# Four PSUM banks in place of two for twelve maxima pieces, and a head mask made earlier, in a decoder block on one core

## The chip, the cores and the metric

One Trainium2 chip, of which the kernel uses one core. The metric is the device time of one execution in microseconds (us). A core has TensorE (PE, matmuls; PEld is its weight load), VectorE (DVE), ScalarE (ACT), GpSimd (POOL) and SyncE (SP, which here only issues DMAs). They run side by side, each through its own list of instructions in order, and meet at semaphores. Matmuls write to PSUM, which has eight banks of 128 x 512 f32.

## The reference

The reference is a decoder block over x (1 x 2048 x 256) with a context of 1601 rows, in f32:

```
h = x @ W_in.T + b_in                      # then a scan over the 2048 positions:
s = s * decay + B_p * h_t ; y_t = C_p * s  # per column, decay = exp(-softplus(log_A))
x = layernorm(x + gamma * norm(y @ W_out.T + b_out) + beta)
q, k, v = x @ Wq, ctx @ Wk, ctx @ Wv       # 8 heads of 64
x = layernorm(x + softmax(q k^T / 8) v @ Wo + bo)
x = layernorm(x + shared_mlp(x) + routed_experts(x))   # 16 experts, top 1
```

## The kernel before

The program has three stages: `before_attention`, `attention`, and the experts with the shared layer. Only the first is touched; it takes about the first 103 us. The attention works on 16 steps (4 chunks of 512 queries by 4 pairs of heads) and subtracts from each score row its maximum. The maxima of a step are found a step ahead, so the maxima for step 0 are made in the first stage, in 32 *pieces*.

In `before_attention` TensorE makes the input projection (L392, 8 groups) while ACT adds the bias (L245) and DVE runs the scan (L320). After that all engines walk through the same list of slots, the function `slots`: 33 slots t = 0, 1, 2, ..., and in each slot each engine does its own part of the named jobs, in a fixed order:

- `out` (t = 0 to 15): the output projection of tile t on TensorE (L403) in banks 2 and 3 by turns; DVE adds the bias (L336, which frees the bank, semaphore `v_z`) and makes the statistics (L338, L339): `norm_a`.
- `norm_b` of tile t - 5 on DVE (L346 to L351), `shifts` (L356), `norm_c` on ACT (L278), `tr`: the transpose of tile t - 12 on TensorE (L439).
- `key` or `val`, one unit per slot for t = 0 to 28, in the order of the list `kv`: slots 0 to 3 keys 0 to 3, slots 4 to 11 values 0 to 7, slots 12 to 15 keys 4 to 7, then keys and values by turns, and keys 13, 14, 15 in slots 26 to 28. Keys go through banks 4 and 5 (L415), ACT rounds them to `K_hi` (L252), DVE subtracts to `K_lo` (L328, `low`), and key n waits for `K_lo` of n - 2 (`v_klo`). Values go through banks 6 and 7 (L426) and ACT copies them out (L257, semaphore `a_v`). The last value is unit 12, in slot 25.
- `query` in slot 16: the query projection of step 0 (L445), `Q_hi` and `Q_alone` on ACT, `Q_lo` on DVE (L363). Before `Q_lo`, DVE makes `mask` (L361): it waits for 32 on `d_ident`, the semaphore of two loads, `ident` (L160) and `wq` (L161), and adds two 128 x 4 strips of `ident`. The mask is first read in the attention stage (L663).
- `piece`: one matmul of 128 x 400 (or 402) on TensorE (L459), and one maximum over it on DVE (L368, `piece_maximum`). From slot 17 on there is a piece ahead of the key or value and one behind it, from slot 24 on (`THREE_FROM`) a third at the slot's end. So slot 26 holds pieces 20, 21, 22, slot 27 pieces 23, 24, 25, slot 28 pieces 26, 27, 28, slot 29 pieces 29, 30, 31.

Pieces alternate between banks 3 (even) and 2 (odd), and piece n waits for the maximum of piece n - 2:

```
if n >= 2:
    pe.wait_ge(v_mx0, n - 1)
pe.matmul(banks[2 + (n + 1) % 2][:, 0:kn], Q_alone[:, h, i * P:(i + 1) * P], ...
```

When all 32 maxima are made, DVE reduces them to `nm` (L374). TensorE goes over to the attention's list: the query projection of step 1 (L773, which waits for `K_lo` of key 15), then the transpose of `nm` (L760, which waits for L374). `M` on DVE (L663) and the first scores (L806) come from it.

The SP queue issues the loads of this stage in this order: `w_in`, `xT`, `w_out`, the four rows, `wk`, `ctxT`, `xring`, `wv`, `xring`, `ident`, `wq`.

Of the kernel before, what the change touches and what calls it, by code (L numbers as in the profile page):

```python
# [9 lines left out]
ALU = mybir.AluOpType  # L10
ACT = mybir.ActivationFunctionType
AX = mybir.AxisListType

P = 128
# [5 lines left out]
KT = (KEYS + P - 1) // P  # L20
LAST = KEYS - (KT - 1) * P
HEADS, DH = 8, 64
# [4 lines left out]
QT = QC // P  # L27
# [5 lines left out]
KC = [(0, 402), (402, 400), (802, 400), (1202, 400)]  # L33


def by_head(nm, par):
    return nm[:, par].rearrange("p (h x) -> p h x", h=2)[:, :, 0:QT]


def before_attention(nc, io, mem):  # L40
# [4 lines left out]
    K_hi, K_lo, V, ident = mem["K_hi"], mem["K_lo"], mem["V"], mem["ident"]  # L45
    with ExitStack() as ctx:
        def sb(name, shape, dt=F32):
            return ctx.enter_context(nc.sbuf_tensor(name, shape, dt))

        def sem(name):  # L50
            return ctx.enter_context(nc.semaphore(name))
# [21 lines left out]
        x1T, mxp, nm, wq, mask = mem["x1T"], mem["mxp"], mem["nm"], mem["wq"], mem["mask"]  # L73
        Q_hi, Q_lo = mem["Q_hi"][0], mem["Q_lo"][0]
        Q_alone = sb("Q_alone", [P, 2, QC], F32R)
        banks = [ctx.enter_context(nc.psum_tensor(f"bank_a{i}", [P, 512], F32)) for i in range(8)]
# [4 lines left out]
        d_ident = sem("d_ident")  # L81
# [13 lines left out]
        p_v, a_v = sem("p_v"), sem("a_v")  # L95
# [4 lines left out]
        p_mx0, v_mx0, v_nm0 = sem("p_mx0"), sem("v_mx0"), sem("v_nm0")  # L100
# [6 lines left out]
              + [u for n in range(8, KT) for u in (("k", n), ("v", n))] + [("k", n) for n in range(KT, 16)])  # L107
        PIECES = TILE_U * len(KC)
        THREE_FROM = 24

        def slots(out=None, key=None, val=None, norm_b=None, shifts=None, norm_c=None, tr=None, query=None, piece=None,
                  low=None):


            def do(f, n, end):
                if f and 0 <= n < end:
                    f(n)

            pieces = iter(range(PIECES))
            for t in range(len(kv) + 4):  # L120
                do(out, t, TILES)
                if t == 16:
                    do(query, 0, 1)
                do(norm_b, t - 5, TILES)
                if t % 4 == 1:
                    do(shifts, (t - 9) // 4, G)
                do(norm_c, t - 10, TILES)
                do(tr, t - 12, TILES)
                if t > 16:
                    do(piece, next(pieces, -1), PIECES)  # L130
                if t < len(kv):
                    kind, u = kv[t]
                    do(key if kind == "k" else val, u, 16)
                if t > 16:
                    do(piece, next(pieces, -1), PIECES)
                if t < len(kv) and kv[t][0] == "k":
                    do(low, kv[t][1], 16)
                if t >= THREE_FROM:
                    do(piece, next(pieces, -1), PIECES)
# [153 lines left out]
        def vector_part(dve):  # L293
            links = [0]

            def link(ins):
                links[0] += 1
                ins.then_inc(v_link, 1)
                dve.wait_ge(v_link, links[0])

            dve.wait_ge(d_cols, 16)
            dve.wait_ge(a_exp, 1)
            dve.tensor_tensor(bB[:], cols[:, 0], cols[:, 2], ALU.mult).then_inc(prep, 1)

            dve.tensor_scalar(decay[:, 1], decay[:, 0], 1.0, None, ALU.add).then_inc(prep, 1)
            dve.wait_ge(prep, 2)
            dve.reciprocal(decay[:, 2], decay[:, 1]).then_inc(prep, 1)

            dve.wait_ge(prep, 3)
            for n in range(8):  # L310
                c, e = n // 2, n % 2
                if n == SCALE_AT:
                    dve.wait_ge(d_rows, 80)
                    for k in range(DK):
                        dve.tensor_scalar(w_out[:, k], w_out[:, k], cols[:, 3, k:k + 1], None, ALU.mult).then_inc(prep, 1)
                dve.wait_ge(a_u, n + 1)
                if c:
                    dve.wait_ge(v_scan, n - 1)
                u = state[:, e, c * 512:(c + 1) * 512]
                dve.tensor_tensor_scan(u, decay[:, 2, e:e + 1].to_broadcast([P, 512]), u,  # L320
                                       state[:, e, c * 512 - 1:c * 512] if c else 0.0,
                                       ALU.mult, ALU.add).then_inc(v_scan, 1)

            def key_low(n):
                p, j = kunits[n]
                k0, kn = KC[j]
                dve.wait_ge(a_khi, n + 1)
                dve.tensor_tensor(K_lo[:, p, k0:k0 + kn], banks[4 + n % 2][:, 0:kn], K_hi[:, p, k0:k0 + kn].bitcast(F32),  # L328
                                  ALU.subtract).then_inc(v_klo, 1)

            def norm_a(t):

                if t == 0:
                    dve.wait_ge(d_rows, 80)
                dve.wait_ge(p_out, t + 1)
                dve.tensor_tensor(z[:, t], banks[2 + t % 2][:, 0:D], rows[:, 0, :], ALU.add).then_inc(v_z, 1)  # L336
                dve.wait_ge(v_z, t + 1)
                link(dve.bn_stats(stats[:, t % 4, 0, :], z[:, t]))  # L338
                dve.bn_aggr(mv[:, 0, t], stats[:, t % 4, 0, :]).then_inc(v_mv1, 1)  # L339

            def norm_b(t):

                if t % 4 == 0:
                    dve.wait_ge(g_rstd1, t // 4 + 1)
                dve.wait_ge(g_xb, t + 1)
                link(dve.scalar_tensor_tensor(z[:, t], z[:, t], mv[:, 0, t, 0:1], rows[:, 1, :], ALU.subtract, ALU.mult))  # L346
                dve.scalar_tensor_tensor(z[:, t], z[:, t], rstd[:, 0, t:t + 1], xring[:, (t // 4) % 2, t % 4],
                                         ALU.mult, ALU.add).then_inc(v_b, 1)
                dve.wait_ge(v_b, t + 1)
                link(dve.bn_stats(stats[:, t % 4, 1, :], z[:, t]))  # L350
                dve.bn_aggr(mv[:, 1, t], stats[:, t % 4, 1, :]).then_inc(v_mv2, 1)  # L351

            def shifts(g):
                dve.wait_ge(g_rstd2, g + 1)
                tiles = slice(4 * g, 4 * g + 4)
                dve.scalar_tensor_tensor(shift[:, tiles], mv[:, 1, tiles, 0], -1.0, rstd[:, 1, tiles], ALU.mult, ALU.mult  # L356
                                         ).then_inc(v_shift2, 1)

            def query_low(_):
                dve.wait_ge(d_ident, 32)  # L360
                dve.tensor_tensor(mask[:], ident[:, 0:QT], ident[:, DH:DH + QT], ALU.add).then_inc(mem["v_mask"], 1)  # L361
                dve.wait_ge(a_q0, 3)
                dve.tensor_tensor(Q_lo[:], banks[1][:], Q_hi[:].bitcast(F32), ALU.subtract).then_inc(v_q0, 1)  # L363

            def piece_maximum(n):
                dve.wait_ge(p_mx0, n + 1)
                u, j = n // len(KC), n % len(KC)
                dve.tensor_reduce(mxp[:, 0, u, j:j + 1], banks[2 + (n + 1) % 2][:, 0:KC[j][1]], AX.X, ALU.max  # L368
                                  ).then_inc(v_mx0, 1)

            slots(out=norm_a, low=key_low, norm_b=norm_b, shifts=shifts, query=query_low, piece=piece_maximum)
            dve.wait_ge(v_mx0, PIECES)
            dve.wait_ge(g_const, 2)
            dve.tensor_reduce(by_head(nm, 0), mxp[:, 0].rearrange("p (h i) j -> p h i j", h=2), AX.X, ALU.max, negate=True  # L374
                              ).then_inc(v_nm0, 1)
            dve.wait_ge(v_nm0, 1)

        def tensor_part(pe):
# [69 lines left out]
            def piece(n):  # L448

                u, j = n // len(KC), n % len(KC)  # L450
                h, i = u // QT, u % QT
                k0, kn = KC[j]
                if n == 0:
                    pe.wait_ge(v_z, TILES)
                    pe.wait_ge(a_q0, 3)
                    pe.wait_ge(a_khi, len(KC))
                if n >= 2:
                    pe.wait_ge(v_mx0, n - 1)
                pe.matmul(banks[2 + (n + 1) % 2][:, 0:kn], Q_alone[:, h, i * P:(i + 1) * P], K_hi[:, 0, k0:k0 + kn],  # L459
                          start=True, stop=True).then_inc(p_mx0, 1)  # L460

            slots(out=out_proj, key=key, val=val, tr=transpose, query=query, piece=piece)

        return sync_part, gpsimd_part, scalar_part, vector_part, tensor_part


# [1470 lines left out]
```

## Time and profile before

| what | value |
|---|---|
| median of 3 runs | 881.26 us (881.13 to 881.49) |
| the profiled execution: its own time | 881.37 us |
| its span in the trace | 879.6 us |
| granted TensorE clock over the span | 0.995 |
| PE busy | 855.2 us (97%) |
| DVE busy | 568.5 us (65%) |
| ACT busy | 363.2 us (41%) |
| POOL busy | 562.8 us (64%) |

All times below count from the start of the span. A row of the timeline gives the start, the length, the engine, the line, the output and the input; "x4" says that four instructions are merged in it, and the bracket at its end gives the idle time of the engine just before and what ended it. A PE row's length includes a pipeline's end that overlaps with the next matmul. Rows of windows give, for each engine, its busy time and its number of instructions in the stretch.

### The profile page before, as it was taken

What the parts mean: (1) busy time and instruction counts of PE and PEld (TensorE: products, weight loads), DVE (VectorE), ACT (ScalarE), POOL (GpSimd) and SP (SyncE); (2) the same over time, 40 slices, a digit from 0 to 9 for tenths busy, and PEclk for the clock granted to TensorE, in tenths of its full rate; (3) what the DMA queues carried; (4) which work ended last, traced back from release to release, by engine and by line L of the source; (5) the groups of instructions that cost most, each with busy time, mean ns of one, the idle gap of its engine ahead of it and who ended that gap; (6) DMA issues with size and microseconds to landing.
All of it is one profiled execution on the core that took longest, in us unless ns stands there. A gap on an engine that the chain in (4) does not pass through costs nothing.

```text
span 879.6 us, 12720 instructions
## 1 busy us (share of the span) xinstructions
PE 855.2 (97%) x4798; PEld 505.5 (57%) x4798; DVE 568.5 (65%) x1149; ACT 363.2 (41%) x510; POOL 562.8 (64%) x366
## 2 busy tenths in 40 slices
PE   9998899999999999999999999999999999999994
PEld 4654555555555455555455556554478898885441
DVE  4798757667666677676677675774677746335553
ACT  3254344434435445443445443544446224323332
POOL 0354298898896898896988986989400153333444
PEclk9999999999999999999999999999999999999998
DMA  9213300000001100000100000104079211484420
GB/s 266 76 48 99 118 1 1 25 1 1 1 1 36 37 1 1 1 1 3 45 25 1 1 1 1 48 1 168 7 178 354 92 49 49 144 282 121 130 71 23
DMA packets 44140, 55.12 MB, mean 63 GB/s; under 512 B 3624, under 2 KB 35120, under 8 KB 44080
## 3 DMA queue, kind: packets, MB, share of 16 engines
q1 hardware_dynamic: 37840, 46.16, 16.7%
q0 software_dynamic: 2688, 6.31, 2.0%
q10 hardware_dynamic: 3552, 1.84, 0.7%
q8 instruction: 39, 0.64, 0.3%
q14 instruction: 21, 0.17, 0.1%
HBM read 36.44 MB, written 18.89 MB: 63 GB/s over the span
## 4 chain that ended last, share of the span: by engine, by line
PE 90%; DVE 7%; issue 1%; POOL 1%; ACT 1%; POOLq 0%; DVEq 0%
PE st L806 24%; PE av L828 21%; PE mx L792 8%; PE bg L1442 4%; PE bu L1442 4%; PE bt L1451 4%; PE bgu L1731 3%; PE misc L773 3%; PE misc L845 2%; PE bank_a L392 2%; PE bank_a L415 1%; PE bgu L1728 1%; PE br L1451 1%; PE mx L859 1%; PE misc L859 1%; PE by L1731 1%
## 5 line engine op out<-in xcount | busy, mean ns | idle before, releaser
L611 POOL TENSOR_TENSOR accG<-accG,probs 128x1024 f32<-128x1024 f32 (+1 forms) x170 | 405.0, 2383 | 38.8 <-ACT probs L633 23.8
L633 ACT ACTIVATE probs<-st 128x1024 f32<-128x1024 f32 (+1 forms) x208 | 212.6, 1025 | 203.2 <-PE st L806 197.5
L678 DVE TENSOR_REDUCE mxp<-mx 128x1 f32<-128x512 f32 x360 | 232.0, 686 | 60.1 <-PE mx L792 54.5
L828 PE MATMUL av<-probs,V 128*64 128x512 f32 (+1 forms) x832 | 191.7, 598 | 0.0
L792 PE MATMUL mx<-K_hi,Q_hi 64*128 64x512 f32 (+1 forms) x480 | 137.9, 380 | 0.0
L828 PEld LDWEIGHTS av<-probs,V 128*64 128x64 f32 (+1 forms) x832 | 55.5, 136 | 105.7 <-issue 83.9
L806 PE MATMUL st<-Q_hi,K_hi 64*128 64x512 f32 (+1 forms) x416 | 112.9, 444 | 0.9 <-ACT probs L633 0.9
L792 PEld LDWEIGHTS mx<-K_hi,Q_hi 64*128 64x128 f32 x480 | 73.8, 184 | 51.8 <-issue 26.8
L806 PE MATMUL st<-M,ones_r 64*128 64x512 f32 (+1 forms) x416 | 101.2, 393 | 0.0
L806 PE MATMUL st<-Q_hi,K_lo 64*128 64x512 f32 (+1 forms) x416 | 96.6, 393 | 0.0
L806 PE MATMUL st<-Q_lo,K_hi 64*128 64x512 f32 (+1 forms) x416 | 94.5, 394 | 0.0
L806 PEld LDWEIGHTS st<-Q_hi,K_hi 64*128 64x128 f32 (+1 forms) x416 | 48.2, 179 | 46.3 <-ACT probs L633 31.3
L693 DVE RECIPROCAL misc<-misc 128x128 f32<-128x128 f32 x64 | 61.4, 960 | 6.3 <-PE misc L845 6.3
L611 POOL TENSOR_TENSOR accG<-probs 128x1024 f32<-128x1024 f32 x16 | 38.4, 2397 | 27.5 <-ACT probs L633 27.5
L806 PEld LDWEIGHTS st<-M,ones_r 64*128 64x128 f32 (+1 forms) x416 | 50.8, 180 | 7.5 <-DVE M L663 0.7
L806 PEld LDWEIGHTS st<-Q_lo,K_hi 64*128 64x128 f32 (+1 forms) x416 | 49.5, 181 | 3.8
L806 PEld LDWEIGHTS st<-Q_hi,K_lo 64*128 64x128 f32 (+1 forms) x416 | 47.5, 180 | 6.2
L1129 POOL DMA_INDIRECT scratch_sorted_x<-x2s,pos x16 | 17.0, 1060 | 37.6 <-DVE pos L1286 23.7
L1442 PE MATMUL bg<-x2T_high,wgate_cut 128*128 128x512 f32 x128 | 40.2, 395 | 0.3 <-DVE h_raw L1312 0.3
L1442 PE MATMUL bu<-x2T_high,wup_cut 128*128 128x512 f32 x128 | 40.0, 394 | 0.0
L675 DVE TENSOR_REDUCE mxp<-mx 128x4 f32<-128x264 f32 x30 | 11.7, 431 | 39.0 <-PE mx L792 39.0
L638 ACT ACTIVATE o_raw<-av 128x512 f32<-128x512 f32 x16 | 9.6, 597 | 60.8 <-PE av L828 60.8
(259 smaller groups left out, 1305.7 us busy)
## 6 DMA issues: line engine op xcount, KB each, us to landing
w_gate_up<-in_gate_up SPq DMA_DIRECT2D x4, 2048.0 KB
w_down<-in_down SPq DMA_DIRECT2D x2, 2048.0 KB, 9.6
scratch_sorted_x<-zero SPq DMA_DIRECT2D x6, 514.0 KB, 8.2
xs<-scratch_sorted_x SPq DMA_DIRECT2D x24, 128.5 KB, 2.3
scratch_base<-zero SPq DMA_DIRECT2D x6, 512.0 KB, 9.4
base<-scratch_base SPq DMA_DIRECT2D x24, 128.0 KB, 2.1
xring<-in_x SPq DMA_DIRECT2D x4, 512.0 KB, 8.9
scratch_x1b<-xT SPq DMA_DIRECT2D x4, 512.0 KB, 2.9
```

The source lines that it names most:

```text
L392: mm = pe.matmul(banks[n % 2][:], w_in[:, k, e * P:(e + 1) * P], xT[:, k, c * 512:(c + 1) * 512], start=(k == 0), stop=(k == DK - 1))
L611: pool.tensor_tensor(total[0:r], so_far[0:r], probs[0:r, place(S, t)], ALU.add).then_inc(g_add, 1)
L633: act.activation(probs[0:r, place(S, t)], st[g % 2][0:r, :], ACT.Exp, scale=DH ** -0.5).then_inc(a_probs, 1)
L678: dve.tensor_reduce(mxp[:, F % 2, h * QT + i, j:j + 1], mx[h][:, 0:kn], AX.X, ALU.max).then_inc(v_mx, 1)
L693: dve.reciprocal(misc[:, cols], misc[:, cols]).then_inc(v_rsum, 1)
L773: mm = pe.matmul(misc[:], wq[:, k, pair * P:(pair + 1) * P], x1T[:, k, :], start=(k == 0), stop=(k == DK - 1))
L792: mm = pe.matmul(mx[h][:, a * kn:(a + 1) * kn], Q_hi[F % 2][rows, q * P:(q + 1) * P], K_hi[rows, F % PAIRS, k0:k0 + kn], start=True, stop= ...
L806: mm = pe.matmul(st[g % 2][0:r, h * QC:(h + 1) * QC], w, q, start=(part == 0), stop=(part == MAXIMA))
L828: mm = pe.matmul(av[h * DH:(h + 1) * DH, :], V[0:r, t, (2 * p + h) * DH:(2 * p + h + 1) * DH], probs[0:r, place(S, t), h * QC:(h + 1) * QC ...
L1442: mm = pe.matmul(bank[f % 2][:], wp[:, k, f * P:(f + 1) * P], xp[:, k, cols], start=(k == n == 0), stop=(k == DK - 1 and n == len(products ...
L1451: return pe.matmul(sum_bank(c * QT + i)[:, 0:D], h, (wd_high, wd_low, wd_high)[n][:, f, :], start=(f == n == 0), stop=(f == FK - 1 and n = ...
L1731: pe.matmul(out[0:HALF, 0:cols], rows_T[:, k * P:k * P + HALF], chosen_rows, start=(k == 0), stop=(k == DK - 1))
```

## The change

Two edits in `before_attention`.

1. Pieces 20 to 31 go round the banks 6, 7, 3, 2 in place of 3 and 2. Piece 20 waits until all 13 values are copied out of banks 6 and 7 (`a_v`); pieces 22 to 31 wait for the maximum of piece n - 4 in place of n - 2. Pieces 0 to 19 are as before.
2. The mask, with its wait for `d_ident`, is made by DVE ahead of the slots, so right behind the scan and ahead of `norm_a` of tile 0, in place of in slot 16.

```diff
         THREE_FROM = 24
+        FOUR_FROM = 20
+
+        def piece_bank(n):
+            return banks[2 + (n + 1) % 2] if n < FOUR_FROM else banks[(6, 7, 3, 2)[n % 4]]
...
             def query_low(_):
-                dve.wait_ge(d_ident, 32)
-                dve.tensor_tensor(mask[:], ident[:, 0:QT], ident[:, DH:DH + QT], ALU.add).then_inc(mem["v_mask"], 1)
                 dve.wait_ge(a_q0, 3)
...
-                dve.tensor_reduce(mxp[:, 0, u, j:j + 1], banks[2 + (n + 1) % 2][:, 0:KC[j][1]], AX.X, ALU.max
+                dve.tensor_reduce(mxp[:, 0, u, j:j + 1], piece_bank(n)[:, 0:KC[j][1]], AX.X, ALU.max
                                   ).then_inc(v_mx0, 1)
 
+            dve.wait_ge(d_ident, 32)
+            dve.tensor_tensor(mask[:], ident[:, 0:QT], ident[:, DH:DH + QT], ALU.add).then_inc(mem["v_mask"], 1)
             slots(out=norm_a, low=key_low, norm_b=norm_b, shifts=shifts, query=query_low, piece=piece_maximum)
...
-                if n >= 2:
+                if n == FOUR_FROM:
+                    pe.wait_ge(a_v, KT)
+                if n >= FOUR_FROM + 2:
+                    pe.wait_ge(v_mx0, n - 3)
+                elif 2 <= n < FOUR_FROM:
                     pe.wait_ge(v_mx0, n - 1)
-                pe.matmul(banks[2 + (n + 1) % 2][:, 0:kn], Q_alone[:, h, i * P:(i + 1) * P], K_hi[:, 0, k0:k0 + kn],
+                pe.matmul(piece_bank(n)[:, 0:kn], Q_alone[:, h, i * P:(i + 1) * P], K_hi[:, 0, k0:k0 + kn],
                           start=True, stop=True).then_inc(p_mx0, 1)
```

## Rows read from the trace of the kernel before

**Rows 1.** The page: the chain that ended last, shares of the span.

```profile
PE 90%; DVE 7%; issue 1%; POOL 1%; ACT 1%; POOLq 0%; DVEq 0%
```

**Rows 2.** DVE's timeline, from the scan's end to the first norm_b.

```profile
22.47 0.42 DVE L336 TENSOR_TENSOR xT<-bank_a,x 128x256 f32<-128x256 f32 x1
...
24.29 0.58 DVE L328 TENSOR_TENSOR K_lo<-bank_a,K_hi 128x402 fp32r<-128x402 f32 x1 [0.71 <-ACT K_hi L252]
...
33.81 0.42 DVE L336 TENSOR_TENSOR xT<-bank_a,x 128x256 f32<-128x256 f32 x1 [1.32 <-PE bank_a L403]
...
34.83 0.48 DVE L346 SCALAR_TENSOR_TENSOR xT<-xT,mv,x 128x256 f32<-128x256 f32 x1
```

**Rows 3.** TensorE's timeline, key 1, output projection 2 and key 2.

```profile
24.41 1.51 PE L415 MATMUL bank_a<-ctxT,wk 128*128 128x400 f32 x4
25.75 1.02 PE L403 MATMUL bank_a<-w_out,state 128*128 128x256 f32 x4
26.62 1.51 PE L415 MATMUL bank_a<-ctxT,wk 128*128 128x400 f32 x4
```

**Rows 4.** The DMA queue's timeline, and issues with KB and us to landing.

```profile
19.27 0.44 SPq L161 DMA_DIRECT2D wq<-in_wq x1
```

```profile
wq<-in_wq SPq DMA_DIRECT2D x1, 512.0 KB, 8.5
ident<-in_ident SPq DMA_DIRECT2D x1, 64.0 KB, 12.8
```

**Rows 5.** DVE's and POOL's timelines: a small DVE operation alone, and the mask.

```profile
6.68 0.16 DVE L303 TENSOR_TENSOR bB<-cols 128x2 f32<-128x2 f32 x1 [6.68 <-ACT decay L240]
...
23.57 5.59 POOL L207 TENSOR_TENSOR xring<-xring,x 128x256 f32<-128x256 f32 x8 [20.59 <-DMA xring<-in_x]
...
65.13 0.56 DVE L361 TENSOR_TENSOR mask<-ident 128x4 f32<-128x4 f32 x1
65.61 0.68 DVE L363 TENSOR_TENSOR Q_lo<-bank_a,Q_hi 128x512 fp32r<-128x512 f32 x1
```

**Rows 6.** TensorE's timelines, matmuls and weight loads: slot 16 and the pieces' end.

```profile
66.44 0.41 PE L439 MATMUL bank_a<-ident,xT 128*128 128x128 f32 x2 [2.46 <-DVE Q_lo L363]
...
91.65 0.19 PEld L459 LDWEIGHTS bank_a<-K_hi,Q_alone 128*128 128x128 f32 x1 [0.50 <-DVE mxp L368]
91.95 1.50 PE L415 MATMUL bank_a<-ctxT,wk 128*128 128x400 f32 x4
92.98 0.84 PE L459 MATMUL bank_a<-K_hi,Q_alone 128*128 128x400 f32 x2
...
94.30 0.45 PE L459 MATMUL bank_a<-K_hi,Q_alone 128*128 128x400 f32 x1 [0.26 <-DVE mxp L368]
...
101.32 1.88 PE L773 MATMUL misc<-x1T,wq 128*128 128x512 f32 x4
103.03 0.27 PE L760 MATMUL mx<-ident,nm 128*128 128x128 f32 x1
```

**Rows 7.** ACT's and DVE's timelines, slots 25 to 29.

```profile
90.84 0.59 ACT L257 ACTIVATE V<-bank_a 65x512 f32<-65x512 f32 x1 [1.75 <-PE bank_a L426]
...
93.67 0.57 DVE L368 TENSOR_REDUCE mxp<-bank_a 128x1 f32<-128x400 f32 x1 [0.95 <-PE bank_a L459]
94.16 0.56 DVE L328 TENSOR_TENSOR K_lo<-bank_a,K_hi 128x400 fp32r<-128x400 f32 x1
...
102.13 0.19 DVE L374 TENSOR_REDUCE nm<-mxp 128x8 f32<-128x32 f32 x1
```

**Rows 8.** Windows of 1 us: length, PE, PEld, DVE, ACT, POOL busy, PEclk, DMA share, GB/s.

```profile
65.00:66.00 1.00, 0.00 (x0) 0.00 (x0) 1.00 (x3) 0.53 (x2) 1.00 (x2) 1.00 0.00 0
867.00:868.00 1.00, 0.87 (x8) 0.30 (x4) 0.70 (x3) 0.00 (x0) 0.70 (x2) 1.00 0.11 38
870.00:871.00 1.00, 0.00 (x0) 0.00 (x0) 0.16 (x1) 0.04 (x1) 0.72 (x1) 0.90 0.18 66
```

**Rows 9.** TensorE's timeline: the first matmuls of the run.

```profile
1.24 4.64 PE L381 MATMUL bank_a<-nm 128*128 128x256 f32 x10 [1.24 <-POOL nm L183]
```

## The prediction

> **What bounds the kernel now.** I read the chain that ended last first. It lies 90% on TensorE and 7% on DVE [rows 1]. The attention and the experts are TensorE's, and the change does not touch them; they follow the first stage at a fixed distance, since their first scores hang on the transpose of `nm`, which starts at 103.03 us [rows 6]. So the question is only by how much that transpose moves.
>
> Then I read the engines' timelines of the first 103 us, and found three stretches with different limits.
>
> From 21 to 34 us TensorE sets the pace. It goes without a pause through output projections and keys, 2.21 us from key 1 to key 2 [rows 3], and DVE waits in each slot: 0.71 us before K_lo of key 0, 1.32 us before norm_a of tile 5 [rows 2].
>
> From 33.81 us, when norm_a of tile 5 starts, to about 80 us DVE runs without any idle time (its rows carry no bracket there), and TensorE is held by DVE, by 2.46 us before the transpose in slot 16 [rows 6]. What delays norm_a of tile 5 delays all of this, and what DVE saves in it comes back.
>
> From about 86 us both engines wait for each other in turn: TensorE for a maximum ahead of the first piece of a slot (0.50 us of idle weight load at 91.65), DVE for the piece behind the key (0.95 us at 93.67) [rows 6, 7]. That is the latency of a loop over two banks, not work.
>
> **The mask's wait, step by step.** Today DVE goes from the last scan straight into norm_a of tile 0, at 22.47 [rows 2]. The change puts a wait for both loads of `d_ident` there. The later is `wq`: issued at 19.27, landed 8.5 us on, so at 27.77; `ident` takes 12.8 us in a queue that moves it no sooner than 26.4 [rows 4]. Today the same wait stands in slot 16 and costs nothing. So DVE will stand still from 22.47 to about 27.85 (0.06 to 0.08 for the semaphore). Queued behind it are norm_a of tile 0 and K_lo of key 0, and TensorE waits for both: output projection 2 needs the bank that norm_a of tile 0 frees, key 2 the one that K_lo of key 0 frees. TensorE still has output projection 1 and key 1 to do, which end at 24.41 + 1.51 = 25.92 [rows 3]. That much of the stall is covered, the rest is not.
>
> The mask itself: bounds are 0.16 us, the length of a small operation with nothing beside it, and 0.48, from 65.13 to the next operation in slot 16, where POOL's adds ran beside it [rows 5]. At 27.8 POOL is adding too (23.57 to 29.16) [rows 5], so I take 0.48. norm_a of tile 0 starts its first operation at 27.85 + 0.48 = 28.33, and that ends 0.42 later, at 28.75. TensorE starts output projection 2 at 28.81 (0.06 for the semaphore) in place of 25.75, so 3.06 us late. DVE then needs 1.02 us for norm_a (33.81 to 34.83) and 0.58 for K_lo of key 0 [rows 2]: 28.33 + 1.02 + 0.58 = 29.93, and key 2 starts at 29.99 in place of 26.62, 3.37 us late. From there TensorE is the slower one again: output projection 3, 1.34 later at 31.33, finds its bank free since 30.25, and key 3, due at 32.20, finds K_lo of key 1 done at 31.43. So the delay stays 3.37, and norm_a of tile 5 starts at 37.18 in place of 33.81. The 1.32 us that DVE idles before it can't take it up, because that wait is for TensorE, which is late by the same amount; from there on DVE has no idle time to give back. **Term 1: +3.37 us** (3.05 with the small mask).
>
> POOL's first inverse square root needs norm_a of tile 3, done at about 33.9, and is through well before 38.2, when norm_b of tile 0 wants it. The second pair of `xring` loads waits for norm_b and shifts with it; SP has nothing else that waits for DVE.
>
> **The mask taken out of slot 16.** 65.13 to 65.61 is 0.48 us of DVE's unbroken stretch, right ahead of `Q_lo`, for which TensorE waits [rows 5, 6]. **Term 2: -0.48 us**; bounds 0 and 0.48.
>
> **Four banks for pieces 20 to 31.** Times here are those of the kernel before, without the shift. Piece 20, at 91.65 now, will wait for the last value's copy, 90.84 + 0.59 = 91.43 [rows 6, 7], and start at 91.49. Its key follows 0.30 later, piece 21 another 1.03 later [rows 6], at 92.82. A slot now takes 2.65 us (91.65 to 94.30), with the 0.50 of idle weight load in it [rows 6]; each piece now asks for a maximum two further back, so that wait falls away, and the slot takes 2.14. DVE needs 0.49 for a maximum and about as much for a K_lo (93.67 to 94.16) [rows 7], so 1.96 a slot. The two are nearly equal, and the end is DVE's. The maximum of piece 21 comes 0.69 behind it as now (92.98 to 93.67), at 93.51. Piece 24 starts at 94.96, its maximum at 95.65; piece 27, a slot later that has no transpose and so takes about 2.0, at 96.97, its maximum at 97.66. Behind that DVE has no wait left: K_lo of key 15 and maxima 28 to 31. Maximum 31 starts at 97.66 + 5 x 0.49 = 100.11 and ends 0.57 later at 100.68; `nm` runs from 100.71 for 0.19 us [rows 7] to 100.90, and the transpose starts at 100.96. TensorE's query projection needs K_lo of key 15 (98.7) and then 1.71 us (101.32 to 103.03) [rows 6], so it is through before. 103.03 - 100.96 gives **Term 3: -2.07 us**. Bounds: if DVE never waited after 93.51, 13 x 0.49 would bring maximum 31 to 99.88, so 2.3; if half of what TensorE gains comes back as waits for DVE, 1.0.
>
> The stores of `x1b` that the first exponent waits for hang on the last transposes, which move as little as piece 20 does; SP has seen them landed by 99.8 already now, so they are covered, by some 3 us.
>
> **Sum.** 3.37 - 0.48 - 2.07 = +0.82 us. The profiled execution took 881.37 (span 879.6 and 1.8 around it), so it would take 882.19; it lies 0.11 above the median, so the median would be 882.1.
>
> **The clock in the gap.** Between key 1 and output projection 2 TensorE will stand idle from 25.92 to 28.81, 2.89 us. The longest such gap now is 2.46 us before 66.44, and the granted clock reads 1.00 in it, the 2.4 GHz level [rows 6, 8]. After the last matmul, which ended at 867.87, it fell to the 1.2 GHz level within the window 870 to 871, whose mean is 0.90, so at about 870.8, after 2.9 us [rows 8]. The Trainium skill (TensorE: Matmul & The Clock Gate, "Part 1: The HAM clock gate") says that half rate is the default state and that activity lifts it, so that an idle array falls back. By it the stall could cost more than its length; by the row of 66.44 it costs only that.
>
> **Rivals.**
>
> *The clock falls in the gap* (18%). For: 2.9 us at the end of the span was enough. Against: 2.46 us was not, and this gap is only as long as the one that just sufficed. Price: TensorE sets the pace right behind it. At the start of the run ten matmuls took 4.64 us, 0.46 each, where four of the same shape later take 1.02, 0.26 each [rows 9, 3]; so the low level lasted at least those 4.6 us, and half of them, 2.3 us, is what such a spell costs; one of half that length costs 1.2. That adds up to 883.3 to 884.4. It decides from 0.9 us of loss on: then the kernel is slower by over 0.2%.
>
> *The stall counts whole* (7%): nothing covers it, 28.33 - 22.47 = 5.86 in place of 3.37, so 884.6. For: DVE is late by that. Against: TensorE has work until 25.92, and DVE waits for it in every slot [rows 2, 3].
>
> *The four banks bring little* (10%): DVE becomes the bound at once, or banks 6 and 7 are free later; term 3 is -1.0, and the time 883.1. Against: DVE's 0.95 us of idle at 93.67 [rows 7].
>
> *The stall is short* (7%): the load of `wq` lands when the scan ends, or soon after. Then only the gain is left, 881.26 - 2.1 = 879.2; with half of the stall, 880.7. Against: 27.77 in this trace [rows 4].
>
> **How the numbers follow.** The forecast holds 58%. 0.2% is 1.76 us, about what a measurement of this kernel can tell from no change. Its own range: landing half a microsecond either way, mask 0.16 to 0.48, term 3 from -2.3 to -1.5, so 881.0 to 883.2. The range of 8 in 10 takes in the clock's case, so 880.7 to 884.5. Slower than 883.0: the clock 18, the whole stall 7, half of the little banks, a tip of the forecast, so 31%. Faster than 879.5: 5%. The rest, 64%, is within.
>
> **What would show it.** In the changed trace: the mask at about 27.8 with an idle bracket of over 5 us before it, ended by the load of `wq`; output projection 2 near 28.8 and key 2 near 30.0; norm_a of tile 5 near 37.2; the transpose in slot 16 2.9 us later than now; the rows of the pieces in slots 27 to 29 with no bracket; DVE unbroken from the maximum of piece 27 to `nm`; the transpose of `nm` near 103.85. The lengths of the matmuls from 28.8 to 34 tell whether the clock fell, even if its column does not. The prediction is wrong if the wait ends elsewhere than 27 to 28.5, if norm_a of tile 5 is not 3.4 late, or if the stages behind the transpose change their distance.

## The result and the profile after

The changed kernel takes 884.59 us (median of 6 runs, 883.23 to 885.97), before 881.29 (881.13 to 881.61) on the same chip: a ratio of 1.0032, 95% interval 1.0022 to 1.0042. It is slower, by 3.3 us by the two medians and by 2.8 by the ratio. The forecast was 882.1, with "within 0.2%" (883.0 or less) as the likeliest; that likeliest outcome did not come. The time lies at the upper end of the range of 880.7 to 884.5 (the median is 0.1 above it, the ratio puts it at 884.1, inside), where the rival with the falling clock had its place. The profiled execution took 884.75, with a span of 882.9. Of all runs below one is in a slower state, 896.79 us at a mean clock of 0.942, and is left aside.

DVE's timeline of the kernel after, the stretch of [rows 2]:

```profile
28.22 0.70 DVE L374 TENSOR_TENSOR mask<-ident 128x4 f32<-128x4 f32 x1 [6.08 <-DMA wq<-in_wq]
28.84 0.41 DVE L340 TENSOR_TENSOR xT<-bank_a,x 128x256 f32<-128x256 f32 x1
...
29.85 0.54 DVE L332 TENSOR_TENSOR K_lo<-bank_a,K_hi 128x402 fp32r<-128x402 f32 x1
...
39.41 0.42 DVE L340 TENSOR_TENSOR xT<-bank_a,x 128x256 f32<-128x256 f32 x1 [1.32 <-PE bank_a L407]
```

The mask stands behind 6.08 us of waiting for `wq`. norm_a of tile 5 is at 39.41 in place of 33.81 [rows 2]: 5.60 us late, not 3.37. (In the eight profiled executions that have no stall this operation starts anywhere from 33.36 to 34.63, so a lateness against the one profile of before is good to about half a microsecond. Distances inside one trace, such as from the mask to norm_a of tile 5, don't carry this scatter.) TensorE's timeline of the same stretch, and windows of 1 us (columns as in [rows 8]):

```profile
24.77 1.51 PE L419 MATMUL bank_a<-ctxT,wk 128*128 128x400 f32 x4
29.40 1.10 PE L407 MATMUL bank_a<-w_out,state 128*128 128x256 f32 x4 [3.12 <-DVE xT L340]
30.45 3.04 PE L419 MATMUL bank_a<-ctxT,wk 128*128 128x400 f32 x4
33.28 1.31 PE L407 MATMUL bank_a<-w_out,state 128*128 128x256 f32 x4
34.42 1.51 PE L419 MATMUL bank_a<-ctxT,wk 128*128 128x400 f32 x4
```

```profile
29.00:30.00 1.00, 0.60 (x3) 0.58 (x4) 0.93 (x4) 0.00 (x0) 0.58 (x1) 1.00 0.00 0
30.00:31.00 1.00, 1.00 (x4) 0.60 (x3) 0.97 (x3) 0.00 (x0) 0.00 (x0) 0.71 0.00 0
31.00:32.00 1.00, 1.00 (x3) 0.39 (x2) 0.96 (x4) 0.00 (x0) 0.00 (x0) 0.50 0.00 0
32.00:33.00 1.00, 1.00 (x3) 0.62 (x2) 0.80 (x3) 0.00 (x0) 0.00 (x0) 0.50 0.00 0
33.00:34.00 1.00, 1.00 (x4) 0.60 (x3) 0.00 (x0) 0.48 (x1) 0.00 (x0) 0.58 0.00 0
```

TensorE was idle for 3.12 us. The gap is over at 29.40, and the granted clock still reads 1.00 there; it falls to the 1.2 GHz level at about 30.4 and returns at about 33.8. Key 2 lies in that spell and takes 3.04 us where key 3 takes 1.51.

The end of the pieces, TensorE's and DVE's timelines, where [rows 6, 7] stood before:

```profile
97.01 0.45 PE L467 MATMUL bank_a<-K_hi,Q_alone 128*128 128x402 f32 x1
97.30 1.51 PE L419 MATMUL bank_a<-ctxT,wk 128*128 128x400 f32 x4
98.34 0.84 PE L467 MATMUL bank_a<-K_hi,Q_alone 128*128 128x400 f32 x2
...
102.35 1.80 PE L467 MATMUL bank_a<-K_hi,Q_alone 128*128 128x400 f32 x5
104.27 1.96 PE L781 MATMUL misc<-x1T,wq 128*128 128x512 f32 x4
106.41 0.30 PE L768 MATMUL mx<-ident,nm 128*128 128x128 f32 x1 [0.19 <-DVE nm L378]
```

```profile
102.11 1.52 DVE L370 TENSOR_REDUCE mxp<-bank_a 128x1 f32<-128x400 f32 x3
103.56 0.56 DVE L332 TENSOR_TENSOR K_lo<-bank_a,K_hi 128x400 fp32r<-128x400 f32 x1
104.04 2.01 DVE L370 TENSOR_REDUCE mxp<-bank_a 128x1 f32<-128x402 f32 x4
106.08 0.19 DVE L378 TENSOR_REDUCE nm<-mxp 128x8 f32<-128x32 f32 x1
```

No piece waits any more, DVE runs through to `nm`, and the transpose of `nm` now waits for it (0.19 us). It starts at 106.41, 3.38 us later than the 103.03 of [rows 6], and the span is 3.3 us longer: nothing behind it changed its distance.

So the place of the time can be followed by four marks of the two traces: norm_a of tile 5 +5.60 (39.41 against 33.81), the transpose that waits for `Q_lo` +5.11 (71.55 against 66.44; it is the first work of slot 17, and what the prediction calls the transpose in slot 16), the last value +5.53 (94.45 against 88.92), the transpose of `nm` +3.38. I use the distance from the last value to that transpose for the banks (14.11 before, 11.96 after), and the one from norm_a of tile 5 to the last value for the stretch that DVE bounds (55.11 before, 55.04 after).

### The profile page after: what moved, and what is told of

Its sections match the earlier page's. It is cut to its first block, busy times and chain, and to the rows that moved or that the text cites. A ratio compares the mean times of both kernels' runs of the same rounds, so it can differ in the third digit from the quotient of the medians.

```text
span 882.9 us, 12720 instructions
## 1 busy us (share of the span) xinstructions
PE 856.7 (97%) x4798; PEld 506.0 (57%) x4798; DVE 568.2 (64%) x1149; ACT 363.4 (41%) x510; POOL 563.1 (64%) x366
## 4 chain that ended last, share of the span: by engine, by line
PE 86%; DVE 8%; SPq 2%; issue 1%; DMA 1%; ACT 1%; POOL 1%; POOLq 0%; DVEq 0%
PE st L814 24%; PE av L836 21%; PE mx L800 8%; PE bg L1450 4%; PE bu L1450 4%; PE bt L1459 4%; PE bgu L1739 3%; PE misc L781 3%; PE misc L853 2%; PE bgu L1736 1%; PE br L1459 1%; PE mx L867 1%; PE misc L867 1%; PE by L1739 1%; PE bank_a L419 1%
## 5 line engine op out<-in xcount | busy, mean ns | idle before, releaser
L800 PEld LDWEIGHTS mx<-K_hi,Q_hi 64*128 64x128 f32 x480 | 73.9, 184 | 51.9 <-issue 26.8
```

What stands on the lines that cost most here:

```text
L800: mm = pe.matmul(mx[h][:, a * kn:(a + 1) * kn], Q_hi[F % 2][rows, q * P:(q + 1) * P], K_hi[rows, F % PAIRS, k0:k0 + kn], start=True, stop= ...
```

## The experiments

Twelve kernels ran in three groups of four, each group on one chip beside the kernel before: its median was 881.80 us in the first group, 881.54 in the second, 881.62 in the third. "Fillers" are matmuls of L381's kind, on zeros and with results that nothing reads, put in where TensorE would stand idle (the trace shows each of these f32 matmuls as two, so six as x12):

```diff
+            def fill(times):
+                for _ in range(times):
+                    pe.matmul(banks[7][:, 0:D], nm[:, 0], nm[:, :, :].rearrange("p a n -> p (a n)"), start=True, stop=True)
```

### The two edits one at a time

**The four banks alone:**

```diff
             def query_low(_):
+                dve.wait_ge(d_ident, 32)
+                dve.tensor_tensor(mask[:], ident[:, 0:QT], ident[:, DH:DH + QT], ALU.add).then_inc(mem["v_mask"], 1)
                 dve.wait_ge(a_q0, 3)
...
-            dve.wait_ge(d_ident, 32)
-            dve.tensor_tensor(mask[:], ident[:, 0:QT], ident[:, DH:DH + QT], ALU.add).then_inc(mem["v_mask"], 1)
```

> The four banks alone, the mask left in slot 16. In the changed kernel the delay against before shrinks from 5.53 us at the last value to 3.38 us at the transpose of nm, so the banks give 2.15 us. Theory (the two edits add up): 881.3 - 2.15 = 879.1 us, transpose of nm near 100.9, granted clock full throughout. Rival (the banks only caught up time that the stall had lost, because DVE was bunched up): under 0.5 us gained, 880.8 or more.

Measured: 879.58 us (12 runs, 878.88 to 882.42), ratio 0.9974 (0.9964 to 0.9984), 2.2 us less than before. From the last value (89.36) to the transpose of `nm` (101.32) it is 11.96, as in the changed kernel. The banks' gain is their own. The clock fell once in this execution, behind a gap of 2.45 us in slot 17, and this time it cost nothing that the marks show (55.10 us from norm_a of tile 5 to the last value, 55.11 before):

```profile
66.88 0.41 PE L443 MATMUL bank_a<-ident,xT 128*128 128x128 f32 x2 [2.45 <-DVE Q_lo L367]
...
67.31 3.34 PE L430 MATMUL bank_a<-wv,ctxT 128*128 128x512 f32 x4
```

```profile
68.00:69.00 1.00, 1.00 (x3) 0.48 (x2) 0.94 (x3) 0.00 (x0) 0.81 (x2) 0.50 0.30 94
```

**The early mask alone,** pieces on two banks (the second edit applied to the kernel before):

> The early mask alone, pieces on two banks. Theory: the loss of norm_a of tile 5 (5.60 us in the changed kernel) less 0.49 for the freed slot 16, plus the 0.42 that DVE loses between slots 16 and 25: about +5.4, so 886.7 us, with a spread over the runs of 2 us or more as in the changed kernel, where before spreads 0.5. Rival (the loss is only the late load, without a clock effect): +3.4 to +3.9, so 885.0, spread 0.5.

Measured: 886.60 us (5 runs, 885.34 to 886.81), ratio 1.0047 (1.0034 to 1.0061), so +4.8 us in medians and +4.1 by the ratio, on five runs. The last value starts at 94.29, the distance to the transpose (108.40) is again 14.11, and its windows show the clock at 0.53, 0.50, 0.50, 0.77 from 30 to 34 us. +4.8 and -2.2 make +2.6; the changed kernel came to +2.8 (884.36 against 881.54) in the second group. The edits add up, within the half microsecond that these numbers allow. The spread, on which the expectation had leaned, is no sign of anything: that of the kernel before was 3.35 us on this chip.

### Is it the clock or the stall?

**The first gap filled:**

```diff
             def out_proj(t):
                 pe.wait_ge(v_scan, 2 * (t // 4 + 1))
+                if t == 2:
+                    for _ in range(6):
+                        pe.matmul(banks[7][:, 0:D], nm[:, 0], nm[:, :, :].rearrange("p a n -> p (a n)"), start=True, stop=True)
```

> The changed kernel with six more matmuls of the kind of L381 (128x256, on zeros, into bank 7, which is free then) between key 1 and output projection 2, to fill TensorE's gap; their results are not used. They take about 2.6 us of the gap of 3.1 us, so by themselves they cost nothing. Theory (the gap lets the granted clock fall, and slow matmuls cost 1.8 us behind it): clock 1.00 throughout, key 2 takes 1.51 us in place of 3.04, time 882.8 us with a spread of 0.6 or less. Rival (the stall's own length makes the whole loss): 884.6 us, no less, and the spread stays.

Measured: 883.38 us (12 runs, 882.28 to 884.82), ratio 1.0018 (1.0010 to 1.0027). The gap is filled, and TensorE's timeline has key 2 at its full speed:

```profile
25.52 2.75 PE L406 MATMUL bank_a<-nm 128*128 128x256 f32 x12
28.69 1.13 PE L410 MATMUL bank_a<-w_out,state 128*128 128x256 f32 x4 [0.41 <-DVE xT L340]
29.83 1.61 PE L422 MATMUL bank_a<-ctxT,wk 128*128 128x400 f32 x4
```

The median is 0.6 above the 882.8 of the theory, and the interval touches that of the changed kernel, so the trace carries this and not the time. The spread stayed, and in the profiled execution the clock fell later, from 75.0 to 78.4 us. That is behind a gap of 2.17 us before piece 2, which nobody had asked about.

**The changed kernel again,** for its spread and for the chip:

> The changed kernel unaltered, on the same chip as the next three. Theory (the clock falls in its first gap in most executions and in the gaps of slots 17 and 18 in some): 884.6 us, spread 2 us or more; it shows how the chip differs from the one of the first comparison.

Measured: 884.36 us (all twelve runs), ratio 1.0029 (1.0020 to 1.0037). Without 896.79 its eleven runs fall in two heaps, four from 882.56 to 883.21 and seven from 884.30 to 885.18. The profiled execution is one of the low heap. The program is that of the first profile, so only the execution and the chip differ. Its TensorE timeline:

```profile
28.43 1.10 PE L407 MATMUL bank_a<-w_out,state 128*128 128x256 f32 x4 [2.87 <-DVE xT L340]
29.48 1.61 PE L419 MATMUL bank_a<-ctxT,wk 128*128 128x400 f32 x4
30.93 1.03 PE L407 MATMUL bank_a<-w_out,state 128*128 128x256 f32 x4
```

The same gap, 0.25 us shorter at 2.87 us, and no fall behind it; key 2 takes 1.61. Its mask ran 0.99 us earlier (27.23 against 28.22, the landing of `wq`), norm_a of tile 5 came 2.63 earlier (36.78 against 39.41), so 1.64 is the clock. That this is what parts the two heaps is not shown: no high run of this series was profiled, and the mean clock over a run, which is on record for each, doesn't part them (0.991 to 0.994 in the low heap, 0.990 to 0.992 in the high one).

In slot 18 it is the other way round. A gap of 2.17 us stands before piece 2 in both executions. In the first the clock stayed at 1.00 behind it, and the key after it took 1.50; here it fell (0.50 from 75 to 78 us), and the key took 2.23. The first profile:

```profile
76.44 0.45 PE L467 MATMUL bank_a<-K_hi,Q_alone 128*128 128x400 f32 x1 [2.17 <-DVE mxp L370]
76.72 1.50 PE L419 MATMUL bank_a<-ctxT,wk 128*128 128x400 f32 x4
```

This one:

```profile
73.86 0.45 PE L467 MATMUL bank_a<-K_hi,Q_alone 128*128 128x400 f32 x1 [2.17 <-DVE mxp L370]
74.14 2.23 PE L419 MATMUL bank_a<-ctxT,wk 128*128 128x400 f32 x4
```

So the same gap in the same program keeps the clock in one execution and loses it in another. In the two profiles that kept it (this program's first and that of the early mask alone) the clock had already fallen once, at 30 us; whether that plays a part is not shown.

**All three gaps filled in the changed kernel:**

```diff
                 pe.wait_ge(v_scan, 2 * (t // 4 + 1))
+                if t == 2:
+                    fill(6)
...
                 if t == QT + 1:
+                    pe.wait_ge(a_v, 8)
+                    fill(5)
                     pe.wait_ge(v_q0, 1)
...
                     pe.wait_ge(a_khi, len(KC))
+                if n == 2:
+                    fill(3)
```

> The changed kernel with filling matmuls in all three gaps: six before output projection 2, five ahead of the transpose in slot 17, three ahead of piece 2; on zeros, into bank 7, results not used. Theory (with the clock held, what is left is the stall of 3.4 to 3.8, the banks' 2.15, and nothing from slot 16): the kernel before with held clock took 881.45, so 882.7 to 883.1, spread 1 us or less; the changed kernel without fillers 1.4 us more. Rival (the stall costs its full length whatever the clock does): 884.4 or more.

Measured: 883.17 us (11 runs, 882.30 to 884.18), ratio 1.0015 (1.0006 to 1.0024), with ten of the runs within 1.2 us. The changed kernel without fillers had 1.0029, so holding the clock gives back about 1.2 us in the median. The two intervals touch and the chips differ; the mean clock of the runs speaks for it too, 0.9915 over the eleven without fillers and 0.9946 over the eleven with them. norm_a of tile 5:

```profile
28.09 0.75 DVE L374 TENSOR_TENSOR mask<-ident 128x4 f32<-128x4 f32 x1 [5.95 <-DMA wq<-in_wq]
```

```profile
37.66 0.42 DVE L340 TENSOR_TENSOR xT<-bank_a,x 128x256 f32<-128x256 f32 x1 [1.32 <-PE bank_a L413]
```

37.66 with the mask at 28.09 is 3.85 us late against before. In the first profile the mask was 0.13 later and norm_a of tile 5 was 5.60 late, so the clock cost 1.62 there, the same as by the other pair.

**The kernel before with the fillers** of slots 17 and 18:

> The kernel before with filling matmuls in the two longest gaps of TensorE: five ahead of the transpose in slot 17 (gap 2.46 us) and three ahead of piece 2 (gap 1.74 us), on zeros, into bank 7, results not used. Theory (the scatter of 880.6 to 884.0 us of the kernel before on the last chip comes from executions in which the clock falls in these gaps, as it did at 67 us in the profile of the four banks alone): the high values of 882.4 and more go, the rest stays at 881.3 to 881.6. Rival (the scatter comes from the DMAs or elsewhere): the spread is as that of before.

Measured: 881.45 us (11 runs, 880.88 to 882.45), ratio 0.9997 (0.9988 to 1.0006). The fillers do what they are for: of the 31 runs of the kernel before beside it 16 have a mean clock of 0.992 or 0.993, with fillers none is below 0.994. But the median doesn't move, so in this kernel the falls cost nothing in most runs. Three of the 31 were at 883.64 to 883.79, and with fillers there is none above 882.45; three in 31 are too few for none in 11 to say anything.

### How long a stall costs what?

**The mask waits for `ident` alone:**

```diff
-            sp.dma_start(ident[:], io["ident"]).then_inc(d_ident, 16)
+            sp.dma_start(ident[:], io["ident"]).then_inc(d_id, 16)
...
-            dve.wait_ge(d_ident, 32)
+            dve.wait_ge(d_id, 16)
```

(with the fillers of slots 17 and 18, and the other waits split in the same way)

> The changed kernel where the mask, still ahead of tile 0, waits for the load of ident alone (a semaphore of its own), fillers in slots 17 and 18, none in the first gap. ident landed at 26.3 in the changed kernel's trace, wq at 28.2. Theory (the stall is set by the landing, and TensorE hides what lies before 25.9): the mask at 26.3, output projection 2 at about 27.4, 1.6 us late, key 2 1.9 late, gap of 1.5 us and no fall of the clock in it: 881.45 + 1.9 - 2.4 = 881.0, within 0.4. Rival (a wait of any length there costs a fall of the clock): 882.5 or more.

Measured: 881.84 us (11 runs, 880.99 to 884.30), ratio 1.0002 (0.9993 to 1.0011). `ident` landed at 26.8 in this execution, 0.5 later than I had put it:

```profile
26.85 0.62 DVE L374 TENSOR_TENSOR mask<-ident 128x4 f32<-128x4 f32 x1 [4.97 <-DMA ident<-in_ident]
```

```profile
27.95 1.10 PE L411 MATMUL bank_a<-w_out,state 128*128 128x256 f32 x4 [1.74 <-DVE xT L340]
29.00 1.61 PE L423 MATMUL bank_a<-ctxT,wk 128*128 128x400 f32 x4
```

A gap of 1.74 us, key 2 at full speed, norm_a of tile 5 at 36.30, 2.49 late: 881.45 + 2.49 - 2.15 = 881.8, which is the measured time, 0.4 above the range expected, and below the rival. Against the kernel with all gaps filled (mask at 28.09, norm_a of tile 5 3.85 late) a stall that ends 1.24 us earlier costs 1.36 less, and neither has a clock effect.

**The load of `ident` moved ahead of `w_out`,** with its own semaphore, no fillers:

```diff
+            sp.dma_start(ident[:], io["ident"]).then_inc(d_id, 16)
             sp.dma_start(w_out[:], io["w_outT"].rearrange("(k p) n -> p k n", p=P)).then_inc(d_rows, 16)
```

> The changed kernel with ident loaded right before w_out and with a semaphore of its own, so that the mask waits for ident alone and finds it there at 22.4. Theory (the whole loss hangs on the wait): the mask takes 0.2 to 0.6 us of DVE, which mostly disappears in the 0.71 us that DVE waits for K_hi of key 0; slot 16 gives 0.49, the banks 2.15; 881.3 - 2.6 + 0 to 0.4 = 878.7 to 879.1. Rival (putting the mask ahead of tile 0 costs its own time on the path from the scan): 879.3 or more. A second rival: the load moved forward delays w_out and the rows, and the scale of w_out and norm_a of tile 0 come later.

Measured: 879.92 us (12 runs, 879.11 to 883.41), ratio 0.9982 (0.9971 to 0.9993). The stall is gone, and the mask costs next to nothing:

```profile
21.62 0.14 DVE L374 TENSOR_TENSOR mask<-ident 128x4 f32<-128x4 f32 x1
21.69 0.43 DVE L340 TENSOR_TENSOR xT<-bank_a,x 128x256 f32<-128x256 f32 x1
```

0.07 us, where beside POOL's adds it took 0.62 (28.22 to 28.84). The median is 0.8 us above what I expected, and in the range of the rival; five of the twelve runs are at 880.67 or more. The profiled run is one of these. In it key 0 waited 1.33 us for `ctxT`, norm_a of tile 5 came at 34.63, and the clock fell behind a gap of 2.17 us (0.50 from 73 to 75 us; 55.59 us from norm_a of tile 5 to the last value). A kernel that leaves the loads as they were (the mask in slot 5 on two banks, below) had the same wait for `ctxT`, 1.20 us, so it can't be laid to the moved load; whether the moved load costs anything stays open.

**The mask in slot 5,** where DVE idles, with four banks:

```diff
                 if t == 0:
                     dve.wait_ge(d_rows, 80)
+                if t == 5:
+                    dve.wait_ge(d_ident, 32)
+                    dve.tensor_tensor(mask[:], ident[:, 0:QT], ident[:, DH:DH + QT], ALU.add).then_inc(mem["v_mask"], 1)
```

> Four banks, and the mask made in slot 5, ahead of norm_a of tile 5, where DVE idles 1.32 us and both loads landed 5 us before. Theory: no stall, no gap; the four banks give 2.15, slot 16 between 0 and 0.49 (with the mask gone from it, the next operation of DVE took 0.91 in place of 0.47 us in the changed kernel): 878.7 to 879.2 on a chip where before takes 881.3. Rival (the mask in slot 5 delays norm_a of tile 5, since DVE is full from there): 879.2 to 879.6.

Measured: 880.12 us (12 runs, 879.34 to 883.14), ratio 0.9986 (0.9977 to 0.9995). No stall; the mask takes 0.13 us in DVE's idle time. The chip's before is 881.54, so this is only 1.4 us less, and the four banks alone had given 2.2; both the theory and the rival had the time lower. In the profile (879.62 us) the clock falls at 72.0 and is back at 75.4, behind a gap that is longer than before:

```profile
66.02 0.41 PE L444 MATMUL bank_a<-ident,xT 128*128 128x128 f32 x2 [1.93 <-DVE Q_lo L368]
...
70.90 0.45 PE L468 MATMUL bank_a<-K_hi,Q_alone 128*128 128x400 f32 x1 [2.16 <-DVE mxp L373]
71.19 2.04 PE L420 MATMUL bank_a<-ctxT,wk 128*128 128x400 f32 x4
```

With the mask out of slot 16 the gap that ends with `Q_lo` shrinks from 2.46 [rows 6] to 1.93, and the one before piece 2 grows from 1.74 to 2.16.

**The same with fillers:**

> The version with the mask in slot 5 together with the same filling matmuls in slots 17 and 18. Theory: the low values of the version with the mask in slot 5, 878.7 to 879.2, without high ones; spread under 1 us. Rival: no difference from it, or slower by the fillers that run past the wait (up to 0.4 us).

Measured: 879.04 us (7 runs, 878.58 to 879.79), ratio 0.9971 (0.9960 to 0.9982), spread 1.2 us. This is the lowest ratio of all: 2.5 us less than before, 5.3 less than the changed kernel beside it. It is not told apart from the four banks alone without fillers (0.9974, 0.9964 to 0.9984): the second edit, put where it does no harm, gains nothing that these runs show.

### What slot 16 and the number of banks are worth

**The mask in slot 5 on two banks, with fillers:**

> The mask in slot 5 alone, on two banks, clock held: the worth of taking the mask out of slot 16 by itself, against 881.45 for the kernel before with held clock. Theory A (DVE's 0.48 us come back): 880.95. Theory B (POOL's adds beside slot 16 hold the next operation of DVE instead, 0.91 in place of 0.47 us, and nothing comes back): 881.4, and in the trace K_lo of the slot to the norm's statistics 2.41 us apart where it was 2.45.

Measured: 881.53 us (11 runs, 881.01 to 882.38), ratio 0.9998 (0.9989 to 1.0007), against 0.9997 with the mask in slot 16. DVE's timeline in slots 16 and 17, and POOL's beside it:

```profile
65.83 0.68 DVE L364 TENSOR_TENSOR Q_lo<-bank_a,Q_hi 128x512 fp32r<-128x512 f32 x1
66.42 0.92 DVE L349 SCALAR_TENSOR_TENSOR xT<-xT,mv,x 128x256 f32<-128x256 f32 x1
67.38 0.83 DVE L350 SCALAR_TENSOR_TENSOR xT<-xT,rstd,xring 128x256 f32<-128x256 f32 x1
68.24 0.43 DVE L353 BATCH_NORM_STATS2 stats<-xT 128x6 f32<-128x256 f32 x1
```

```profile
65.64 3.15 POOL L222 TENSOR_TENSOR xT<-xT,x 128x256 f32<-128x256 f32 x4
```

From `Q_lo` to the statistics it is 2.41 us; before, from the mask to the statistics, it was 2.45 (65.13 to 67.58). The first operation of norm_b takes 0.92 in place of 0.47. POOL's adds of 0.79 us each run beside both, and the time that the mask had taken longer, norm_b's first operation now takes longer. That is theory B, by the trace; the interval of the time would still hold theory A. That POOL's adds are what both wait for is read from their standing side by side: no run changed POOL.

**Three banks,** mask in slot 5, with fillers:

```diff
-            return banks[2 + (n + 1) % 2] if n < FOUR_FROM else banks[(6, 7, 3, 2)[n % 4]]
+            return banks[2 + (n + 1) % 2] if n < FOUR_FROM else banks[(3, 6, 7)[n % 3]]
...
-                if n >= FOUR_FROM + 2:
-                    pe.wait_ge(v_mx0, n - 3)
+                if n >= FOUR_FROM + 1:
+                    pe.wait_ge(v_mx0, n - 2)
```

> Mask in slot 5, clock held, and pieces 20 to 31 round three banks (3, 6, 7) in place of four: a piece waits for the maximum three back. Theory (the loss of the two banks was the latency of their loop, and one more bank covers it, as DVE is the bound from there on): 879.0 to 879.3, as with four (879.04). Rival (each bank gives its share): half of the 2.4 us, 880.2.

Measured: 879.74 us (11 runs, 879.25 to 882.63), ratio 0.9981 (0.9972 to 0.9990). From the last value (88.75) to the transpose (101.01) it is 12.26, with four banks 11.97 (88.52 to 100.49), with two 14.11. The third bank brings 1.85 of the 2.14, the fourth 0.29, because the last piece still waits with three:

```profile
99.01 0.45 PE L476 MATMUL bank_a<-K_hi,Q_alone 128*128 128x400 f32 x1 [0.52 <-DVE mxp L373]
```

The theory holds in its main part, though the time is 0.4 above its range; the times alone (0.9971 and 0.9981) would not tell three from four.

## Why the prediction came out as it did

The time came out at the upper end of the range, but by a case that I had given 18%: the forecast's own path gives 882.1, and its range ended at 883.2. By one of the prediction's own signs it was wrong, since norm_a of tile 5 was not 3.4 late; the other two (the wait's end, 28.2, and the stages behind the transpose) came as said. Point by point:

- **"The mask's wait, step by step", term 1, +3.37.** The mechanism was right: who waits, what TensorE covers, and that nothing is given back until DVE's stretch. It was 5.60. Of this 3.98 is the stall (3.85 with all gaps filled and the mask at 28.09, and 0.13 for the mask at 28.22): `wq` landed later (mask at 28.22, not 27.85, 0.37), the mask took 0.62 (not 0.48, 0.14), and TensorE started 0.15 behind norm_a's first operation (not 0.06); key 2 came at 30.45, not 29.99, and the rest is a tenth of a microsecond or two behind it. The other 1.62 is the clock. From the mask to norm_a of tile 5 it is 11.19 us in this profile and 11.03 in that of the early mask alone, where the clock fell, and 9.53, 9.55 and 9.57 in the three where it did not: 1.5 to 1.7 us, with nothing taken from the kernel before.
- **"The clock in the gap", by the row of 66.44 the stall "costs only that".** This is the step that failed. A gap of 2.46 us that had kept its clock in one profile was taken for a gap that always keeps it. The runs show that it is a matter of the execution: behind 2.45 us the four banks alone lost it (windows of 0.79 and three of 0.50 from 67 to 71 us), and behind 2.46 the kernel before kept it; behind 2.17 us in slot 18 the changed kernel lost it in one profile and kept it in another. In the first gap it was lost behind 3.12 and 3.08 us and kept behind 2.87; these three alone would also fit a limit on the length. Filled, key 2 ran at full speed in both profiles. The Trainium skill's rule (TensorE: Matmul & The Clock Gate, "Part 1: The HAM clock gate"), that activity lifts the clock and an idle array falls back, was right against my reading of the row: the trace agrees, with 0.50 from 31 to 33 us behind the gap. But the clock read 1.00 through the whole gap and fell a microsecond after work had begun again. The rival's price, 1.2 to 2.3 us, holds the measured 1.6: the spell lasted 3.4 us (30.4 to 33.8) at half the clock. The price had been taken from the lengths of the first matmuls of the run, where the clock's column reads 1.00 (from 1 to 6 us), so the column is no witness there. The chance was too low if anything, with a fall in two of the three profiles that have the long gap unfilled.
- **"The mask taken out of slot 16", term 2, -0.48.** Wrong: 0 to 0.1. The distance from norm_a of tile 5 to the last value is 55.04 after and 55.11 before. I had POOL's adds beside the mask in hand, and used them for the mask's price in its new place, but not for what is freed: where an operation is long only because of something that runs beside it, taking it out can free nothing, since the next one is long instead (0.92 in place of 0.47 us).
- **"Four banks for pieces 20 to 31", term 3, -2.07.** Right: 2.15, alone, with the early mask, and with the mask in slot 5. The details came as said: no brackets, DVE unbroken to `nm`, the transpose waiting for it.
- **The sum.** 3.98 + 1.62 - 0.07 - 2.15 = 3.38, the delay of the transpose; terms of 3.98 - 0.07 - 2.15 = +1.8 without the clock agree with 883.17, which is 1.6 above before. The forecast's sum of +0.82 missed the clock (1.62), 0.61 of stall and 0.41 of slot 16, and gained 0.08 by the banks: nearly all its errors lay on one side, and two thirds of the miss is the term that it put at nothing.
- **Behind the transpose** nothing moved: 776.57 us from it to the end of the span before, 776.49 after, 776.71 in the best version.

What stays open: the few runs 2 to 3 us above the rest, of the kernel before too. With fillers in slots 17 and 18 only two such runs are left in the 62 runs of the six series that have them (882.63 with three banks, 884.30 with the wait for `ident` alone). A single fall in the stretch that DVE bounds isn't enough for them. The distance from norm_a of tile 5 to the last value is 54.99 to 55.21 us in the nine profiles without a fall there; in the five that have one it is 55.10 (four banks alone), 55.23 (mask in slot 5), 55.35 (first gap filled), 55.50 (the changed kernel again) and 55.59 (`ident` moved ahead), so it costs 0 to 0.5. The 93 runs of the kernel before say the same: 33 have a mean clock of 0.992 or less and a median of 881.59, 48 have 0.994 or more and a median of 881.57. All eleven runs above 883.1 have 0.993, and only one other run has that. So the high runs have something to do with when the clock is low, but not simply with how long. No profile caught one of them.

## What to carry to other kernels

Moving an operation moves its wait too, and on an engine in order the wait holds everything behind it: before a move, look up when the data lands, not only what the operation costs. Where an engine that sets the pace would stand idle for two to three microseconds, price the spell at the lower clock that may follow it (here 1.6 us) beside the gap itself, and don't trust one profile that it stays away. The ring of two buffers between two nearly equally busy engines lost its latency each round here; one more buffer brought 1.85 us of 2.14.

## What the runs showed of the hardware

- The granted clock fell behind idle stretches of TensorE of 2.16, 2.17 (three profiles), 2.45 and 3.08 to 3.12 us, and stayed in other executions behind 1.74, 2.17 (two profiles), 2.46 and 2.87 us. In these gaps it fell only when TensorE had started again (at 30.4 with work from 29.40 on, at 67.6 with work from 66.88 on), and stayed at 0.50 for about three microseconds of dense matmuls. At the end of the run it fell in idle time [rows 8].
- With fillers in the gaps of slots 17 and 18 none of six profiles has a fall, and 60 of 62 runs have a mean clock of 0.994 or more; without them seven of eight profiles have one fall each, at 30 us or in one of the two slots.
- Where DVE set the pace, such a spell cost 0 to 0.5 us; where TensorE did, 1.5 to 1.7.
- A 128x4 add on DVE took 0.07 us of its time with POOL idle (21.62 to 21.69), and 0.48 to 0.67 beside POOL's 128x256 adds (28.09 to 28.76 in the changed kernel with fillers).
- `wq`, 512 KB, landed 8.4 or 8.5 us after its issue in all 13 profiles that have the loads in their first order. What scattered was the issue, at 18.82 us in the changed kernel again and at 19.78 in the first profile, behind the issue of `ident`, which took 5.46 to 6.36 us itself; the mask that waits for `wq` ran at 27.23 and 28.22. `ident`, 64 KB, landed 12.2 to 13.1 us after its issue. A wait on the last load of a long queue carries that scatter with it.
